# One maximum and one exponential over two PSUM banks in the attention stages of a four-layer megakernel

## The chip, the cores and the metric

The kernel runs on one core of a Trainium2 chip. The metric is the device time of one execution in microseconds. The engines are TensorE (PE; its weight loads are PEld), VectorE (DVE), ScalarE (ACT), GpSimd (POOL) and SyncE (SP). SBUF is the on-chip memory with 128 partitions; PSUM, which PE writes, is used as eight banks of 512 fp32 values in each partition.

## What is computed

Eight sequences of 128 tokens with 128 features pass four layers, each an attention-like part and a feed-forward part with residuals and layer norms. The change touches the three softmax attentions over a context (16 heads of 8 features). All have this core; they differ in what is added to the scores or multiplied to the weights:

```python
# layer 1 (stage A0)
scores = jnp.einsum('bhqd,bhkd->bhqk', q, k) / jnp.sqrt(jnp.float32(DEPTH)).astype(q.dtype)
attn = jax.nn.softmax(scores, axis=-1)
out = jnp.einsum('bhqk,bhkd->bhqd', attn, v)
# layer 2 (stage A1)
logits = logits + neg[:, None, :, :]          # mask, -1e9 where masked
attn = jax.nn.softmax(logits, axis=-1)
attn = attn * group_prob[:, None, :, :]
# layer 3 (stage A2)
scores = jnp.einsum('bhtd,bhsd->bhts', q, k) + bias   # relative position
weights = jax.nn.softmax(scores, axis=-1)
```

## The kernel before

Instructions of each engine stand in one hand-written order, and engines wait for each other by counting semaphores. An attention stage `a` (0, 1, 2; called A0, A1, A2 here) handles the eight sequences as blocks `b` in turn. The 16 heads of a block are four groups `j` of four heads `g`; a group's 4 x 128 scores fill one PSUM bank, and groups go in pairs `p` (j = 2p and 2p+1).

For each block PE computes the scores twice. `att_rows` (L888) gives them with queries on the partitions, into banks 0 and 1, and `att_max` on DVE (L909) takes the negated row maxima, one instruction for each bank. PE transposes the maxima (`att_max_pe`, L940), and DVE adds them to the queries as extra features (`att_max_dve`, L949, tile QX). `att_cols` (L962) then gives the shifted scores with keys on the partitions, into banks 2 and 3, and `att_exp` on ACT (L980) takes the exponential of each bank into PF. `att_pv` (L997, L1003) sums the weights and multiplies them by the values; `att_norm` divides (REC L1011, AT L1015), `att_out` projects, and `att_x` (L1049) adds the result to X. In A0 and A2 the next layer norm is applied by POOL, in A1 by DVE (XN, L306); in A1 and A2 `turn_one_pe` (L349) transposes each normed block for the next layer.

The stages differ so:

- A0 has no mask. The matmuls of a pair's two banks alternate, so both banks are finished almost together.
- A1 adds a mask by two 512-wide matmuls for each bank, all of bank 0 (or 2) before those of bank 1 (or 3); they are issued by a helper and shown as L187 (NMA, NMB with DGH, DGL). The maximum is split into three fp16 parts by five small DVE instructions (`att_max_split`, L919, L921, L923, L925, L927). POOL multiplies each exponentiated bank by the group probabilities (`att_group`, L984).
- A2 adds a position bias by helper matmuls (L187 with FLIP), one for each bank of scores on the row side and two on the column side.

PE's order in a block is: `att_cols` of pair 0, `att_rows` of the next block's pair 1, `att_pv` of the last block's groups 2 and 3, `att_cols` of pair 1, L940 of the next block, `att_out` of block b-2, `att_rows` of block b+2's pair 0, `att_pv` of groups 0 and 1, and the turn of block b-3. PE already waits for both maxima of a pair before it writes banks 0 and 1 again, and for both exponentials before it writes banks 2 and 3 again.

Of the kernel before, what the change touches and what calls it, by code (L numbers as in the profile page):

```python
# [40 lines left out]
def gated_mix_program(nc, t, out):  # L41
# [5 lines left out]
    with ctx:  # L47
# [5 lines left out]
        def sem(name):  # L53
            if name not in sems:
                sems[name] = ctx.enter_context(nc.semaphore(name))
            return sems[name]
# [845 lines left out]

        def att_max(dve, a, b, u, j):

            n = NB * a + b
            dve.wait_ge(sem("a_rows"), 4 * n + j + 1)
            src = bank(j % 2).rearrange("p (g s) -> p g s", g=4)
            dst = MF[:, 0, 4 * j:4 * j + 4] if a == 1 else MB[:, u, :, 32 * j + 24]
            dve.tensor_reduce(dst, src, AX, ALU.max, negate=True).then_inc(sem("a_max"), 1)  # L909

# [62 lines left out]

        def att_exp(act, a, b, u, j):

            n = NB * a + b
            act.wait_ge(sem("a_cols"), 4 * n + j + 1)
            if n:
                act.wait_ge(sem("a_pv"), 4 * n + j - 3)
            act.activation(PF[:, j, :], bank(2 + j % 2), ACT.Exp).then_inc(sem("a_exp"), 1)  # L980

# [112 lines left out]
        def att_act(act, a):  # L1094
            k, j = NEXT[a]
            for b in range(NB):
                u = b % 2
                for i in range(4):
                    att_exp(act, a, b, u, i)
                if b >= 1:  # L1100
                    att_high(act, a, b - 1, 1 - u)
                if j and b >= 3:
                    turn_one_act(act, j, b - 3)
            att_high(act, a, NB - 1, 1)
            if j:
                for b in range(NB - 3, NB):
                    turn_one_act(act, j, b)

        def att_dve(dve, a):
# [8 lines left out]

            for i in range(4):
                att_max(dve, a, 0, 0, i)  # L1120
            att_max_split(dve, a, 0, 0)
            att_max_dve(dve, a, 0, 0)
            for b in range(NB):
                u, end = b % 2, b == NB - 1
                if not end:
                    att_max(dve, a, b + 1, 1 - u, 0)
                    att_max(dve, a, b + 1, 1 - u, 1)
                if own and b >= 2:
# [3 lines left out]
                if not end:  # L1132
                    att_max(dve, a, b + 1, 1 - u, 2)
                    att_max(dve, a, b + 1, 1 - u, 3)
                    att_max_split(dve, a, b + 1, 1 - u)
# [431 lines left out]
```

## Time and profile before

| what | value |
|---|---|
| median of 3 runs | 828.68 us (827.31 to 829.53) |
| the profiled execution's own time | 829.18 us |
| its span, first to last instruction | 827.4 us |
| mean granted clock of TensorE | 0.862 of full |
| PE busy | 662.5 us (80%) |
| DVE busy | 639.3 us (77%) |
| ACT busy | 363.7 us (44%) |
| POOL busy | 357.8 us (43%) |
| chain that ended last | PE 64%, DVE 20%, POOL 8%, issue 6%, ACT 2% |

The busy times are unions over the whole span, in which projection, attention and expert stages with different limits follow each other. The chain is the sequence of work, followed back from the last instruction, that had to be done in that order for the program to end when it did.

### The profile page before, as it was taken

What the parts mean: (1) busy time and instruction counts of PE and PEld (TensorE: products, weight loads), DVE (VectorE), ACT (ScalarE), POOL (GpSimd) and SP (SyncE); (2) the same over time, 40 slices, a digit from 0 to 9 for tenths busy, and PEclk for the clock granted to TensorE, in tenths of its full rate; (3) what the DMA queues carried; (4) which work ended last, traced back from release to release, by engine and by line L of the source; (5) the groups of instructions that cost most, each with busy time, mean ns of one, the idle gap of its engine ahead of it and who ended that gap; (6) DMA issues with size and microseconds to landing.
All of it is one profiled execution on the core that took longest, in us unless ns stands there. A gap on an engine that the chain in (4) does not pass through costs nothing.

```text
span 827.4 us, 17071 instructions
## 1 busy us (share of the span) xinstructions
PE 662.5 (80%) x5144; PEld 317.1 (38%) x5144; DVE 639.3 (77%) x1199; ACT 363.7 (44%) x630; POOL 357.8 (43%) x642
## 2 busy tenths in 40 slices
PE   1359924999988684878993899999999976997696
PEld 0113312444434463324542344444444432454342
DVE  5558764799977786666886799999999967575696
ACT  1314411888875441332331445555555545333443
POOL 6065624577742155205665244554444420025251
PEclk9755555999997798689996899999999988899799
DMA  8000000121204000000000111111111100000110
GB/s 257 0 0 2 0 0 8 44 55 53 55 27 124 2 3 2 1 0 2 2 2 11 33 53 51 52 55 55 53 50 53 55 13 1 2 3 2 32 54 29
DMA packets 46244, 26.81 MB, mean 32 GB/s; under 512 B 17255, under 2 KB 45207, under 8 KB 46032
## 3 DMA queue, kind: packets, MB, share of 16 engines
q1 hardware_dynamic: 44792, 24.36, 10.6%
q10 hardware_dynamic: 1408, 1.85, 0.6%
q8 instruction: 29, 0.48, 0.2%
q14 instruction: 15, 0.12, 0.0%
HBM read 25.63 MB, written 0.56 MB: 32 GB/s over the span
## 4 chain that ended last, share of the span: by engine, by line
PE 64%; DVE 20%; POOL 8%; issue 6%; ACT 2%; DVEq 0%; POOLq 0%; ACTq 0%
PE PS L187 51%; PE PS L446 4%; POOL RSTD L302 4%; DVE SHARED L875 3%; DVE MB L909 2%; PE PS L997 2%; PE PS L888 2%; PE PS L1003 1%; DVE MF L909 1%; POOL VE L300 1%; DVE STAT L290 1%; DVE REC L1011 1%; PE PS L962 1%; DVE XN L306 1%; PE PS L940 1%
## 5 line engine op out<-in xcount | busy, mean ns | idle before, releaser
L709 ACT ACTIVATE SHARED<-SHARED 128x512 f16<-128x512 f32 x180 | 112.4, 630 | 126.8 <-DVE SHARED L724 122.3
L729 DVE TENSOR_TENSOR SHARED<-SHARED 128x512 f16<-128x512 f32 x180 | 145.8, 830 | 12.6 <-ACT SHARED L709 12.2
L724 DVE TENSOR_TENSOR SHARED<-SHARED,PS 128x512 f32<-128x512 f32 x180 | 120.9, 686 | 11.3 <-ACT SHARED L702 7.3
L187 PE MATMUL PS<-XH,UH 128*128 128x512 f16 x296 | 113.9, 385 | 2.2 <-ACT CT L553 2.2
L187 PE MATMUL PS<-XL,UH 128*128 128x512 f16 x296 | 113.8, 384 | 0.0
L187 PE MATMUL PS<-XH,UL 128*128 128x512 f16 x296 | 113.7, 384 | 0.0
L187 PE MATMUL PS<-SHARED,DNH 128*128 128x512 f16 x360 | 107.1, 379 | 5.4 <-DVE SHARED L729 5.3
L980 ACT ACTIVATE SHARED<-PS 128x512 f32<-128x512 f32 x96 | 52.3, 595 | 99.2 <-PE PS L187 74.2
L720 DVE TENSOR_TENSOR SHARED<-SHARED,PS 128x512 f32<-128x512 f32 x116 | 78.7, 679 | 10.7 <-PE PS L187 10.7
L656 POOL CAST DNH<-DF 128x128 f16<-128x128 f32 x90 | 26.0, 289 | 134.6 <-PE PS L187 134.6
L646 POOL TENSOR_TENSOR UL<-UF,UH 128x256 f16<-128x256 f32 (+1 forms) x90 | 69.4, 771 | 7.2
L187 PE MATMUL PS<-CT,SEL 128*128 128x512 f16 x180 | 69.1, 384 | 0.0
L187 PE MATMUL PS<-SHARED,DNL 128*128 128x512 f16 x180 | 68.3, 379 | 0.0
L699 ACT ACTIVATE SHARED<-PS 128x512 f32<-128x512 f32 x116 | 62.3, 584 | 3.9 <-PE PS L187 3.9
L644 POOL CAST UH<-UF 128x256 f16<-128x256 f32 (+1 forms) x90 | 45.5, 506 | 41.4 <-PE PS L187 39.0
L300 POOL TENSOR_SCALAR VE<-MV 128x1 f32<-128x1 f32 x72 | 15.9, 220 | 104.3 <-DVE MV L296 104.2
L984 POOL TENSOR_TENSOR SHARED<-SHARED,GPT 128x512 f32<-128x512 f32 x32 | 40.0, 1271 | 43.7 <-ACT SHARED L980 43.7
L909 DVE TENSOR_REDUCE MB<-PS 128x4 f16<-128x512 f32 x64 | 41.2, 688 | 19.0 <-PE PS L187 13.9
L187 PEld LDWEIGHTS PS<-SHARED,DNH 128*128 128x128 f16 x360 | 34.6, 97 | 49.7 <-issue 13.4
L658 POOL TENSOR_TENSOR DNL<-DF,DNH 128x128 f16<-128x128 f32 x90 | 48.1, 535 | 7.2
L702 ACT ACTIVATE SHARED<-PS,B 128x512 f32<-128x512 f32 x64 | 43.8, 687 | 6.9 <-PE PS L187 1.9
L187 PEld LDWEIGHTS PS<-XH,UH 128*128 128x128 f16 x296 | 29.2, 99 | 44.2 <-issue 11.7
(260 smaller groups left out, 1248.6 us busy)
## 6 DMA issues: line engine op xcount, KB each, us to landing
UF<-in_up SPq DMA_DIRECT2D x58, 128.0 KB, 2.0
DF<-in_down SPq DMA_DIRECT2D x90, 64.0 KB, 1.8
SEL<-in_sel SPq DMA_DIRECT2D x90, 32.0 KB, 1.7
UF<-in_up SPq DMA_DIRECT2D x32, 64.0 KB, 1.7
SHARED<-t_values_dram SPq DMA_DIRECT2D x2, 1024.0 KB, 10.5
SHARED<-in_masks ACTq DMA_DIRECT2D x1, 1024.0 KB, 10.3
WF<-in_wsmall SPq DMA_DIRECT2D x1, 868.0 KB, 6.2
X<-in_x SPq DMA_DIRECT2D x1, 512.0 KB, 3.7
```

The source lines that it names most:

```text
L187: last = pe.matmul(dst, l, r, start=start and i == 0, stop=stop and i == len(pairs) - 1)
L644: pool.tensor_copy(UH[:, u, 0:n], UF[:, u, 0:n]).then_inc(sem("e_up_ready"), 1)
L646: pool.tensor_tensor(UL[:, u, 0:n], UF[:, u, 0:n], UH[:, u, 0:n], ALU.subtract)\
L658: pool.tensor_tensor(DNL[:, u, :], DF[:, u, :], DNH[:, u, :], ALU.subtract)\
L699: act.activation(SG[:, hf, :], bank(hf), ACT.Silu).then_inc(sem("e_act"), 1)
L702: act.activation(SG[:, hf, :], bank(hf), ACT.Relu, bias=B1[:, bass.ds(c, 1)]).then_inc(sem("e_act"), 1)
L709: act.activation(HHI[:, u, hf, :], HF[:, hf, :], ACT.Copy).then_inc(sem("e_high"), 1)
L720: dve.tensor_tensor(TG[:, hf, :], SG[:, hf, :], bank(2 + hf), ALU.mult).then_inc(sem("e_gated"), 1)
L724: dve.tensor_tensor(HF[:, hf, :], src[:, hf, :], bank(4 + hf), ALU.mult).then_inc(sem("e_hidden"), 1)
L729: dve.tensor_tensor(HLO[:, u, hf, :], HF[:, hf, :], HHI[:, u, hf, :], ALU.subtract).then_inc(sem("e_low"), 1)
L909: dve.tensor_reduce(dst, src, AX, ALU.max, negate=True).then_inc(sem("a_max"), 1)
L980: act.activation(PF[:, j, :], bank(2 + j % 2), ACT.Exp).then_inc(sem("a_exp"), 1)
```

## The change

Each pair of banks is read by one instruction. The maximum waits for both banks' scores, reads 128x1024 values and writes 128x8; the exponential waits for both banks of shifted scores and writes 128x1024. Each raises its semaphore by two. All other instructions, and the order on each engine, stay as they are.

```diff
-        def att_max(dve, a, b, u, j):
+        def att_max(dve, a, b, u, p):
 
             n = NB * a + b
-            dve.wait_ge(sem("a_rows"), 4 * n + j + 1)
-            src = bank(j % 2).rearrange("p (g s) -> p g s", g=4)
-            dst = MF[:, 0, 4 * j:4 * j + 4] if a == 1 else MB[:, u, :, 32 * j + 24]
-            dve.tensor_reduce(dst, src, AX, ALU.max, negate=True).then_inc(sem("a_max"), 1)
+            dve.wait_ge(sem("a_rows"), 4 * n + 2 * p + 2)
+            src = bank(0, 2).rearrange("p (j g s) -> p j g s", j=2, g=4)
+            if a == 1:
+                dst = MF[:, 0, :].rearrange("p (j g) -> p j g", j=4)[:, 2 * p:2 * p + 2, :]
+            else:
+                dst = MB[:, u].rearrange("p g (j c) -> p j g c", j=4)[:, 2 * p:2 * p + 2, :, 24]
+            dve.tensor_reduce(dst, src, AX, ALU.max, negate=True).then_inc(sem("a_max"), 2)
...
-        def att_exp(act, a, b, u, j):
+        def att_exp(act, a, b, p):
 
             n = NB * a + b
-            act.wait_ge(sem("a_cols"), 4 * n + j + 1)
+            act.wait_ge(sem("a_cols"), 4 * n + 2 * p + 2)
             if n:
-                act.wait_ge(sem("a_pv"), 4 * n + j - 3)
-            act.activation(PF[:, j, :], bank(2 + j % 2), ACT.Exp).then_inc(sem("a_exp"), 1)
+                act.wait_ge(sem("a_pv"), 4 * n + 2 * p - 2)
+            act.activation(PF[:, 2 * p:2 * p + 2, :].rearrange("p j n -> p (j n)"), bank(2, 2), ACT.Exp).then_inc(sem("a_exp"), 2)
...
                 if not end:
                     att_max(dve, a, b + 1, 1 - u, 0)
-                    att_max(dve, a, b + 1, 1 - u, 1)
                 if own and b >= 2:
                     att_low(dve, a, b - 2, u)
                 if j and b >= 4:
                     turn_one_dve(dve, j, b - 4)
                 if not end:
-                    att_max(dve, a, b + 1, 1 - u, 2)
-                    att_max(dve, a, b + 1, 1 - u, 3)
+                    att_max(dve, a, b + 1, 1 - u, 1)
```

On DVE, in a middle block of stage A1, the order before has two maxima for each pair, MF being the row maxima, MB their fp16 parts and XL the low half of a turned block:

```order
L909 TENSOR_REDUCE MF<-PS 128x4 [waits a_rows] x2
L1030 TENSOR_TENSOR ATL<-AT,ATH 128x128 [waits a_out,a_at_hi]
L357 TENSOR_TENSOR XL<-PS,XH 128x128 [waits xt_high]
L909 TENSOR_REDUCE MF<-PS 128x4 [waits a_rows] x2
L919 TENSOR_SCALAR MB<-MF 128x4x4 [waits a_max]
L921 SCALAR_TENSOR_TENSOR MF<-MB,MF 128x16 [waits a_msplit]
```

The same place of the changed kernel, whose lines are numbered three higher from here on:

```order
L912 TENSOR_REDUCE MF<-PS 128x8 [waits a_rows]
L1033 TENSOR_TENSOR ATL<-AT,ATH 128x128 [waits a_out,a_at_hi]
L357 TENSOR_TENSOR XL<-PS,XH 128x128 [waits xt_high]
L912 TENSOR_REDUCE MF<-PS 128x8 [waits a_rows]
L922 TENSOR_SCALAR MB<-MF 128x4x4 [waits a_max]
L924 SCALAR_TENSOR_TENSOR MF<-MB,MF 128x16 [waits a_msplit]
```

Nothing changes places; of two instructions in a row one is left, of twice the width. On ACT, in the same stage, four exponentials (PS to PF, which lies in SHARED) stand between the copies of the attention output (ATH) before:

```order
L353 ACTIVATE XH<-PS 128x128 [waits xt_turned]
L980 ACTIVATE SHARED<-PS 128x512 [waits a_pv,a_cols] x4
L1022 ACTIVATE ATH<-AT 128x128 [waits a_out,a_norm]
L353 ACTIVATE XH<-PS 128x128 [waits xt_turned]
L980 ACTIVATE SHARED<-PS 128x512 [waits a_pv,a_cols] x4
```

and in the changed kernel there are two of twice the width:

```order
L353 ACTIVATE XH<-PS 128x128 [waits xt_turned]
L983 ACTIVATE SHARED<-PS 128x1024 [waits a_pv,a_cols] x2
L1025 ACTIVATE ATH<-AT 128x128 [waits a_out,a_norm]
L353 ACTIVATE XH<-PS 128x128 [waits xt_turned]
L983 ACTIVATE SHARED<-PS 128x1024 [waits a_pv,a_cols] x2
```

## Rows read from the trace of the kernel before

**Rows 1.** Windows: us, busy (count) of each engine, clock, DMA.

```profile
272.00:319.00 47.00, 36.13 (x822) 26.27 (x822) 36.63 (x74) 19.34 (x39) 20.45 (x37) 0.85 0.01 3
361.00:446.00 85.00, 69.43 (x966) 36.16 (x967) 61.67 (x145) 22.06 (x48) 48.36 (x52) 0.92 0.01 2
377.00:381.00 4.00, 4.00 (x49) 2.10 (x50) 1.81 (x3) 0.00 (x0) 0.00 (x0) 0.57 0.00 0
397.00:414.00 17.00, 16.39 (x250) 8.76 (x246) 14.24 (x35) 5.29 (x12) 11.09 (x11) 1.00 0.01 2
713.00:752.00 39.00, 39.00 (x670) 22.41 (x668) 27.97 (x58) 14.86 (x33) 8.43 (x17) 1.00 0.01 3
```

**Rows 2.** Groups by line: count, busy us, mean ns, idle before.

```profile
L980 ACT ACTIVATE SHARED<-PS 128x512 f32<-128x512 f32 x96 | 52.3, 595 | 99.2 <-PE PS L187 74.2
L909 DVE TENSOR_REDUCE MB<-PS 128x4 f16<-128x512 f32 x64 | 41.2, 688 | 19.0 <-PE PS L187 13.9
```

**Rows 3.** Single lines: ns min/median/max, first and last start.

```profile
L1237 DVE TENSOR_REDUCE AMX<-XN x1: 1220/1220/1220, 325.5 to 325.5; 128x8 f32<-128x1024 f32 x1
...
L790 ACT ACTIVATE SHARED<-PS x3: 1023/1023/1023, 246.2 to 821.1; 128x1024 f32<-128x1024 f32 x3
...
L923 DVE TENSOR_SCALAR MB<-MF x8: 202/204/1227, 365.2 to 426.9; 128x16 f16<-128x16 f32 x8
```

**Rows 4.** The chain that ended last, in A0: start, us, what.

```profile
302.95 1.19 DVE MB L909 x2
...
304.19 0.44 PE PS L888 x8
```

**Rows 5.** Timeline of PE, one block of A1: start, us, instruction, idle before.

```profile
405.27 0.39 PE L962 MATMUL PS<-QX,SHARED 32*128 32x128 f16 x8
...
406.25 0.38 PE L187 MATMUL PS<-NMB,DGL 128*128 128x512 f16 x1
...
407.65 0.38 PE L187 MATMUL PS<-NMA,DGL 128*128 128x512 f16 x1
...
413.60 0.30 PE L349 MATMUL PS<-EYE,XN 128*128 128x128 f32 x1 [0.18 <-DVE X L1049]
413.84 0.40 PE L962 MATMUL PS<-QX,SHARED 32*128 32x128 f16 x8
```

**Rows 6.** Timeline of ACT, the same block.

```profile
406.24 1.08 ACT L980 ACTIVATE SHARED<-PS 128x512 f32<-128x512 f32 x2 [0.59 <-PE PS L187]
```

**Rows 7.** Timeline of POOL, the same block.

```profile
406.91 2.50 POOL L984 TENSOR_TENSOR SHARED<-SHARED,GPT 128x512 f32<-128x512 f32 x2 [0.52 <-ACT SHARED L980]
410.62 2.50 POOL L984 TENSOR_TENSOR SHARED<-SHARED,GPT 128x512 f32<-128x512 f32 x2 [1.20 <-ACT SHARED L980]
```

**Rows 8.** Timeline of DVE, the same block.

```profile
405.35 1.25 DVE L909 TENSOR_REDUCE MF<-PS 128x4 f32<-128x512 f32 x2
...
407.63 1.29 DVE L909 TENSOR_REDUCE MF<-PS 128x4 f32<-128x512 f32 x2 [0.63 <-PE PS L187]
408.96 0.52 DVE L919 TENSOR_SCALAR MB<-MF 128x16 f16<-128x16 f32 x1
...
411.45 0.42 DVE L949 TENSOR_TENSOR QX<-PS,SHARED 128x512 f16<-128x512 f16 x1
411.78 1.42 DVE L306 TENSOR_SCALAR XN<-X,MV,RSTD 128x128 f32<-128x128 f32 x1
```

**Rows 9.** Timeline of DVE, block 0 of A1.

```profile
373.94 1.23 DVE L923 TENSOR_SCALAR MB<-MF 128x16 f16<-128x16 f32 x1
375.20 1.16 DVE L925 SCALAR_TENSOR_TENSOR MF<-MB,MF 128x16 f32<-128x16 f16 x1
```

**Rows 10.** Timeline of POOL, block 0 of A1.

```profile
373.85 2.48 POOL L984 TENSOR_TENSOR SHARED<-SHARED,GPT 128x512 f32<-128x512 f32 x2 [0.22 <-ACT SHARED L980]
```

**Rows 11.** Timeline of ACT, last block of A2.

```profile
753.25 1.09 ACT L980 ACTIVATE SHARED<-PS 128x512 f32<-128x512 f32 x2 [0.59 <-PE PS L187]
```

**Rows 12.** Timeline of PE, last block of A2.

```profile
754.59 0.40 PE L962 MATMUL PS<-QX,SHARED 32*128 32x128 f16 x8
```

More of the change, by code:

```diff
@@ L1097, in att_act @@
                 u = b % 2
-                for i in range(4):
-                    att_exp(act, a, b, u, i)
+                att_exp(act, a, b, 0)
+                att_exp(act, a, b, 1)
                 if b >= 1:
@@ L1117, in residual @@
                 ln_mean(dve, k, b, b)
-            for i in range(4):
-                att_max(dve, a, 0, 0, i)
+            att_max(dve, a, 0, 0, 0)
+            att_max(dve, a, 0, 0, 1)
             att_max_split(dve, a, 0, 0)
```

## The prediction

> **What bounds the kernel now.** I read the windows first, then the chain that ended last, then the timelines of single blocks. The change touches three attention stages, here A0, A1 and A2 (a = 0, 1, 2); A0 takes 47 and A1 85 us of the 827.4 us span. The windows [rows 1] say that they have different limits. In the middle of A2 PE is busy 39.00 of 39.00 us: it is the bound there, and DVE and ACT have air. In A0 PE is busy 36 of 47 us and DVE 37 of 47, and the chain goes through DVE: two maxima, eight score matmuls [rows 4], two maxima again, then the softmax division, QX and the residual, without a gap. In A1 no engine looks full (PE 69, DVE 62, POOL 48 of 85 us), so a loop of waits has to be looked for.
>
> One block of A1 lasts from the `att_cols` matmuls at 405.27 to those of the next block at 413.84: 8.57 us [rows 5]. In it ACT takes its first two exponentials at 406.24 [rows 6], POOL multiplies them by the group probabilities from 406.91 for 2.50 us, to 409.41, and the other two from 410.62 to 413.12 [rows 7]. On DVE [rows 8] the second pair of maxima begins when its bank's mask products are done (407.63) and ends at 408.92; then comes L919, 0.52 us long, to 409.48; XN (L306) takes 1.42 us, to 413.20; after it come X (L1049) and, 0.18 us idle later, PE's transpose L349 and the next block's L962 [rows 5]. Both long instructions end 0.07 to 0.08 us after a pair of POOL's multiplications. In block 0 of this stage it is plainer: L923, 0.204 us in the median [rows 3], takes 1.23 us from 373.94 and L925 after it 1.16 us to 376.36 [rows 9], while POOL multiplies from 373.85 to 376.33 [rows 10]. Each is let through when one POOL multiplication of 1.24 us ends. So in A1 these DVE instructions wait for POOL, and the loop is: cols, exponentials, POOL's first pair, L919, the split, ..., XN held to the end of POOL's second pair, X, turn, cols. That DVE and POOL block each other here is what the trace shows. The Trainium skill, "SBUF — State Buffer", section "Who interferes with whom", names it: a port pair shared by the two, held for a whole instruction, and asked for by DVE's `tensor_scalar` and by forms with two SBUF inputs, but not by a reduce. By that rule the trace agrees.
>
> **The change, part by part.**
>
> *Size of the wide instruction.* A 512-wide maximum takes 688 ns and a 512-wide exponential 595 ns [rows 2]. The 128x1024 reduce L1237 takes 1220 ns, the 1024-wide activation over two PSUM banks L790 1023 ns [rows 3]. L1237 reads SBUF and the maxima PSUM; I take 1.22 for them too, the nearest row, and L790 read PSUM. Two separate maxima overlap at their ends: a ready pair takes 1.25 us, one that had to wait 1.29 [rows 8], a pair of exponentials 1.08 [rows 6]. So a fused pair saves 0.03 to 0.07 us on DVE and 0.06 on ACT, not the 0.156 (2 x 0.688 - 1.22) that the means suggest. The Trainium skill, "Perfetto Trace Analysis", section "Optimizing Scalar/DVE Operations", puts the engine-busy overhead of a DVE instruction on PSUM at about 125 ns; by it A0's 16 pairs would give 2.0 us back (an estimate) where the rows give under 1. The same section says that where these engines are not saturated and make others wait, splitting instructions can finish work sooner, which speaks against this change.
>
> *A0.* Scores of both banks end almost together (the eight matmuls of rows 4 take 0.44 us, so the last two are 0.05 apart). The first pair of a block saves 0.04; the second starts 0.05 later and still saves 0.03. Over 8 blocks 0.56, less about 0.1 in the first blocks where PE runs slower: **-0.4 us**. The bounds are 0 and -2.5 (16 x 0.156).
>
> *A1, exponentials.* Here bank 2's mask products end two products before bank 3's. The first exponential started at 406.24; the last mask product ends at 406.25 + 0.38 = 406.63, so a fused one starts at 406.67, **0.43** later [rows 5, 6]. POOL's first multiplication waits for the first exponential (0.595) now, and for both (1.023) then: **0.43** more. POOL's pair thus starts and ends **0.86 us later**: 407.77 to 410.27. L919 is then ready at 409.3 and is let go at 410.33 instead of 409.48, so the split, REC, AT and QX all move by 0.85. The second exponentials and POOL's second pair move by the same 0.86, since `att_cols` for it hangs on PE's order and not on DVE. QX ended at 411.87 and the first of that POOL pair ended at 411.87 too (410.62 + 1.25), and XN lost that race; both sides move equally, so I take it that XN loses again and ends at 414.06. X, turn and the next cols follow: the block costs **+0.86**. In blocks 1 and 2 there is no XN yet, but the loop closes through L919, PE's L940, the next row scores and the value products: again +0.86. Block 0 is alike (POOL's two pairs back to back) at about +0.9; in block 7 the four multiplications run back to back from the first exponentials to the final value products: +0.86. Sum 0.9 + 6 x 0.86 + 0.86 = 6.9.
>
> *A1, maxima.* The fused maximum waits for the last mask product: 407.65 + 0.38 = 408.03 in place of 407.63, and ends at 409.27 in place of 408.92, **+0.35**. That hides in all blocks behind the 0.86 at L919 (behind DVE's wait for POOL, that is; without it +0.35 would show). Only block 0's own maxima, ahead of the first exponential, are uncovered: +0.35, less 0.06 for the pair before: +0.3. **A1 in all: +7.2 us.** Queued behind DVE's late maxima are the split and so PE's L940, counted above; queued behind POOL's late pair is ln_rstd, which waits for the residual's mean, itself 0.86 later.
>
> *A2.* The mask here is one product a bank on the row side, 0.22 us (half of the two products' 0.43), so a waiting maximum ends 0.22 - 0.07 = 0.15 later; on the column side it is two, so the pair of exponentials ends 0.43 - 0.06 = 0.37 later. PE waits for neither in the 39 us in which it is full. Exposed are block 0's maxima, when PE has nothing else (+0.15, less 0.05 for the pair before), and the last block: its fused exponentials would begin at 753.25 + 0.43 and end at 754.70 [rows 11], while L962, which needs both, starts at 754.59 [rows 12]: +0.1. **+0.2 us.**
>
> **Sum.** -0.4 + 7.2 + 0.2 = +7.0 us. The profiled execution took 829.18 us, 1.8 of it outside the span, where nothing changes; with the sum it is 836.2. This execution lies 0.5 above the median of 828.68, so **835.7 us** (+0.84%). A measurement of this kernel can tell about 0.3%, 2.5 us.
>
> **The rivals.**
>
> *POOL's delay is free* (0.10). If L919 and XN are long for another reason than POOL, only the late maxima count: 8 x 0.35 - 0.05 x 8 in A1, so 2.4 - 0.4 + 0.2 = +2.2, 830.9 us. For it: it is the plain reading of the chain, which names DVE and not POOL. Against it: four long instructions of rows 8 and 9 each end within 0.08 us of a POOL end.
>
> *The wide maximum saves a whole fixed cost* (0.04). If DVE saves the upper bound, 0.156 a pair, A0 gives 2.5 back instead of 0.4 and A1 and A2 gain nothing, being held elsewhere: 833.6. Against it stands the overlap of the pairs in rows 8. The 125 ns of "Perfetto Trace Analysis" in the Trainium skill is this case, by its own figure.
>
> *XN wins its race* (inside my forecast). If QX ends a hair before POOL's first multiplication, XN no longer waits. PE then becomes the limit: L940 is still 0.86 late and PE loses only its 0.18 us of idle time [rows 5], so +0.68 in four blocks: 835.0.
>
> *The TensorE clock falls* (0.12). In A1's steady part PE is busy 16.39 of 17 us at clock 1.00; just before, 377 to 381, it ran at 0.57, mostly the lower of its two levels (1.2 and 2.4 GHz), after waiting for the split [rows 1]. With 0.86 us more idle in each block such stretches may come again; one costs about 4.00 x 0.43 = 1.7 us. One to three: 837.4 to 840.8. Against it: A0 waits a larger share of its time and is mostly at 1.00 (0.85 over the stage).
>
> *Faster* (0.04): the later PE work falls into stretches of full clock. The low clock costs now (1 - 0.85) x 47 = 7.0 us of clock in A0 and (1 - 0.92) x 85 = 6.8 in A1 [rows 1], partly off the path. If the shifts made it vanish wholly in both, 835.7 - 13.8 = 821.9; it decides from 9.5 us up, more than two thirds of it. What lies ahead of each stage, and so the start of the slow stretches, doesn't change, so this is remote.
>
> **How the numbers follow.** 0.70 for the forecast, whose own range is 834 to 837; 0.10 for POOL's delay free, 0.12 for the clock, 0.04 each for the fixed cost and for faster. The range reaches down to the second and up into the third: 830.5 to 839.0. The chance of no change (within 2.5 us) takes most of POOL's delay free and a little of shifts that cancel, 0.09; faster 0.04; slower 0.87.
>
> **What would show it.** In the changed profile: the maximum at 1.22 us and the exponential at 1.02; in A1 POOL's pair starting 2.50 us after the block's cols in place of 1.64, L919 lasting about 1.0 us and ending 0.07 after POOL, XN still near 1.4 us, blocks of 9.4 us in place of 8.57, PE idle about 0.9 us before L940; A2's blocks unchanged with PE full; A0's blocks 0.07 shorter. Wrong would make it: L919 short while POOL works, exponentials much longer than 1.02 over two banks, a clock under 1.00 in A1's later blocks.

## The result, and the profile after

The changed kernel takes 845.84 us in the median of 6 runs (843.29 to 847.48), the kernel before 829.08 (827.31 to 829.57). The ratio is 1.0203 with an interval of 1.0183 to 1.0223: slower by 16.8 us, where 7.0 were forecast and the range ended at 839.0. The profiled execution of the changed kernel took 847.17 us with a span of 845.4, so 18.0 us more span than the one of before.

The windows of the changed kernel that answer to [rows 1] (two blocks of A1, and the middle of A2; columns as there):

```profile
404.25:422.17 17.92, 15.53 (x235) 8.27 (x233) 14.36 (x29) 4.99 (x7) 10.77 (x10) 1.00 0.01 2
...
728.00:767.00 39.00, 39.00 (x658) 21.93 (x650) 25.96 (x43) 13.08 (x19) 8.43 (x17) 1.00 0.01 2
```

TensorE is still full in the middle of A2 and loses 2.39 of 17.92 us in A1, at full clock. The new instructions, by line (ns min/median/max, first and last start) and from the page's groups (busy, mean ns):

```profile
L922 DVE TENSOR_SCALAR MB<-MF x8: 203/1056/1130, 367.4 to 435.7; 128x16 f16<-128x16 f32 x8
...
L983 ACT ACTIVATE SHARED<-PS 128x1024 f32<-128x1024 f32 x48 | 49.1, 1023 | 104.1 <-PE PS L187 65.3
...
L912 DVE TENSOR_REDUCE MB<-PS 128x8 f16<-128x1024 f32 x32 | 39.2, 1225 | 23.6 <-PE PS L187 17.4
```

Maximum and exponential have the sizes taken from [rows 3]: 1225 and 1023 ns. L922 is the old L919; its median went to 1056 ns. The same block as in [rows 5 to 8], on PE:

```profile
412.74 0.40 PE L965 MATMUL PS<-QX,SHARED 32*128 32x128 f16 x8
...
418.81 0.40 PE L943 MATMUL PS<-EYEH,MB 128*128 128x128 f16 x4 [1.05 <-DVE MB L930]
...
422.17 0.40 PE L965 MATMUL PS<-QX,SHARED 32*128 32x128 f16 x8
```

on ACT:

```profile
414.19 1.02 ACT L983 ACTIVATE SHARED<-PS 128x1024 f32<-128x1024 f32 x1 [1.07 <-PE PS L187]
```

on POOL:

```profile
415.29 2.50 POOL L987 TENSOR_TENSOR SHARED<-SHARED,GPT 128x512 f32<-128x512 f32 x2 [1.43 <-ACT SHARED L983]
418.94 2.50 POOL L987 TENSOR_TENSOR SHARED<-SHARED,GPT 128x512 f32<-128x512 f32 x2 [1.15 <-ACT SHARED L983]
```

and on DVE:

```profile
415.56 1.22 DVE L912 TENSOR_REDUCE MF<-PS 128x8 f32<-128x1024 f32 x1 [1.13 <-PE PS L187]
416.81 1.04 DVE L922 TENSOR_SCALAR MB<-MF 128x16 f16<-128x16 f32 x1
...
419.83 0.41 DVE L952 TENSOR_TENSOR QX<-PS,SHARED 128x512 f16<-128x512 f16 x1
420.16 1.37 DVE L306 TENSOR_SCALAR XN<-X,MV,RSTD 128x128 f32<-128x128 f32 x1
```

The block lasts 422.17 - 412.74 = 9.43 us instead of 8.57. POOL's first pair starts 2.55 us after the block's cols (1.64 before) and ends at 417.79; L922 ends at 417.85, the split's last part (L930) releases L943, and PE has stood idle 1.05 us for it. XN, asked for at 420.16, ends at 421.53, beside POOL's end at 421.44. That is the loop of the prediction, nearly to the hundredth. Eight blocks of it explain less than half of the loss.

**Where the rest is.** Both programs issue the same 5144 matmuls in the same order, so the start of each can be compared. The table gives, for matmuls named by their start in the trace of before, how much later they start in the changed kernel:

| start before | what it is | shift, us |
|---|---|---|
| 45.70 | L411, the 27th matmul, in the first layer | +0.90 |
| 248.12 | end of the first expert stage | +1.18 |
| 273.60 | A0 begins | +2.33 |
| 321.33 | A0 has ended | +2.39 |
| 362.44 | A1 begins | +2.25 |
| 386.07 | L940 of A1's block 2 | +5.67 |
| 441.31 | A1 has ended | +11.02 |
| 666.10 | end of the second expert stage | +11.89 |
| 684.89 | projection ahead of A2 | +11.15 |
| 694.24 | nine us on in that projection | +13.47 |
| 700.43 | A2 begins | +13.36 |
| 750.10 | A2, full part | +16.51 |
| 822.20 | end | +17.99 |

A1 gives 8.8 of it. But 2.3 stand ahead of A1's start, 2.3 between A1 and A2, 3.2 in A2's first block and 1.5 from there to the end. What stands ahead of A1 need not belong to the change: at 45.70 the same matmul is between 1.66 us early and 0.90 late in the traces at hand, and e13 below, which is the kernel before up to the end of A1, enters A1 2.66 us late. A1 has such a scatter too. e4, e13, e14 and e15 leave it as it was and take -0.1, -2.5, -0.1 and +0.5 us for it, against the trace of before; the -2.5 stand in its first block.

Two of these places can be read. The projection ahead of A2, the same 31 matmuls of the changed kernel and then of the kernel before:

```profile
696.05:707.71 11.66, 9.68 (x31) 3.96 (x32) 7.17 (x11) 5.66 (x9) 0.00 (x0) 0.66 0.00 0
```

```profile
684.89:694.24 9.35, 7.35 (x31) 3.43 (x32) 6.54 (x10) 5.29 (x8) 0.00 (x0) 0.83 0.00 0
```

The granted clock was 0.66 here against 0.83, and the same work took 2.31 us more: more of it was done at the lower of TensorE's two levels (1.2 in place of 2.4 GHz). No instruction of this stage differs. In the stretch just ahead of it (from 666.10 to 684.89 in the kernel before) it is the other way round, again the changed kernel first:

```profile
677.99:696.04 18.05, 7.88 (x56) 4.18 (x54) 10.96 (x34) 6.45 (x10) 6.14 (x16) 0.93 0.01 2
```

```profile
666.10:684.89 18.79, 10.56 (x56) 6.33 (x55) 11.06 (x34) 6.45 (x10) 6.14 (x16) 0.81 0.01 2
```

With two levels, full and half, the time at the lower one is twice the missing share of the clock: 2.5 + 7.9 us in the changed kernel and 7.1 + 3.2 before, so about 10 us over both stretches in either (an estimate). The low clock did not last longer here, it lay later. In the first stretch that gave 0.74 us back, in the projection it cost 2.31. The other place is ACT at the start of A2, in the changed kernel:

```profile
721.09 1.28 ACT L983 ACT_TABLE_LOAD   x1 [9.28 <-issue]
722.38 1.02 ACT L983 ACTIVATE SHARED<-PS 128x1024 f32<-128x1024 f32 x1
725.20 1.02 ACT L983 ACTIVATE SHARED<-PS 128x1024 f32<-128x1024 f32 x1 [1.80 <-issue]
```

and in the kernel before:

```profile
698.40 1.28 ACT L980 ACT_TABLE_LOAD   x1
706.19 0.60 ACT L980 ACTIVATE SHARED<-PS 128x512 f32<-128x512 f32 x1 [6.50 <-PE PS L187]
```

ACT loads the function table of the exponential once at this place, 1.28 us. Before, it did so at 698.40, right behind its last projection work and 6.5 us ahead of need. In the changed kernel it idles 9.28 us first, ahead of the load, and the load then stands between the finished scores and the exponential. PE's next `att_cols` waits for it:

```profile
723.46 0.40 PE L965 MATMUL PS<-QX,SHARED 32*128 32x128 f16 x8 [1.58 <-ACT SHARED L983]
```

The trace's full list of ACT instructions shows why. It prints the semaphore instructions too (start, us, operation, line, semaphores waited for by `>=` and raised):

```
kernel before
697.46  0.02 EVENT_SEMAPHORE L979  S[192]>=
698.40  1.28 ACT_TABLE_LOAD  L980
706.19  0.60 ACTIVATE        L980  S[191]>=  S[150]++
changed kernel
710.93 10.13 EVENT_SEMAPHORE L982  S[192]>= S[191]>=
721.09  1.28 ACT_TABLE_LOAD  L983
722.38  1.02 ACTIVATE        L983  S[150]+=
```

S[191] is `a_cols`, S[192] `a_pv`, S[150] `a_exp`. Before, S[191] stands on the exponential itself: the wait for the scores was part of it, behind the table load. In the changed kernel the exponential raises its semaphore by two, carries no wait any more, and both waits lie in an instruction of their own ahead of the table load. The Trainium skill, "Trainium Kernel Development and Optimization", section "Key Constraints", says that compute semaphores are to be raised by 1; it gives no reason, and here the two did work, at this price.

### The profile page after: what moved, and what is told of

The parts are those of the page before. It is cut to its first block and busy times, and to the rows that moved or that the text cites. A ratio compares the mean times of both kernels' runs of the same rounds, so it can differ in the third digit from the quotient of the medians.

```text
span 845.4 us, 16979 instructions
## 1 busy us (share of the span) xinstructions
PE 667.2 (79%) x5144; PEld 316.5 (37%) x5144; DVE 641.6 (76%) x1151; ACT 362.8 (43%) x582; POOL 354.4 (42%) x642
## 5 line engine op out<-in xcount | busy, mean ns | idle before, releaser
L983 ACT ACTIVATE SHARED<-PS 128x1024 f32<-128x1024 f32 x48 | 49.1, 1023 | 104.1 <-PE PS L187 65.3
L646 POOL TENSOR_TENSOR UL<-UF,UH 128x256 f16<-128x256 f32 (+1 forms) x90 | 65.9, 733 | 7.2
L699 ACT ACTIVATE SHARED<-PS 128x512 f32<-128x512 f32 x116 | 62.7, 588 | 5.4 <-PE PS L187 5.4
L912 DVE TENSOR_REDUCE MB<-PS 128x8 f16<-128x1024 f32 x32 | 39.2, 1225 | 23.6 <-PE PS L187 17.4
```

What stands on the lines that cost most here:

```text
L646: pool.tensor_tensor(UL[:, u, 0:n], UF[:, u, 0:n], UH[:, u, 0:n], ALU.subtract)\
L699: act.activation(SG[:, hf, :], bank(hf), ACT.Silu).then_inc(sem("e_act"), 1)
L983: act.activation(PF[:, 2 * p:2 * p + 2, :].rearrange("p j n -> p (j n)"), bank(2, 2), ACT.Exp).then_inc(sem("a_exp"), 2)
```

## The experiments

All ratios are to runs of the kernel before on the same chip, whose medians were 828.83 to 829.76 us.

**One kind of instruction at a time.** e1 fuses only the maxima, e2 only the exponentials, each in all stages; `att_max` or `att_exp` then calls the old form for both banks:

```diff
         def att_exp(act, a, b, p):
+            if a not in ():        # e1; e2 has this in att_max
+                att_exp_one(act, a, b, 2 * p)
+                att_exp_one(act, a, b, 2 * p + 1)
+                return
```

> Only the maxima are fused, in all three stages; every exponential reads one bank as before. Theory (the cost is the late exponentials: POOL's multiplications and with them DVE in A1, a displaced wait and an uncovered table load in A2): in A1 the fused maximum ends at about 0.35 us later, still before POOL's first pair ends, so L919 is let go at the same moment and the blocks stay at 8.57 us; only block 0 pays 0.3; A0 gains 0.4. In all 829 to 830 us. Rival (the maxima's late start is what costs): 8 x 0.35 in A1 and 0.15 in each block of A2, 832 us or more.

Measured: 830.52 us (828.52 to 832.93), ratio 1.0006 [0.9986, 1.0026]. The wide maxima cost nothing that can be measured and gain nothing. A1's blocks were 8.51 us. The theory holds.

> Only the exponentials are fused, in all three stages. Theory: nearly the whole cost of the change, 842 to 846 us, with A1's blocks at 9.4 us and the ACT table load of A2 behind the wait. Rival (both halves of the change are needed for the loss): under 838 us.

Measured: 838.46 us (833.37 to 842.14), ratio 1.0101 [1.0064, 1.0137]. The exponentials alone cost 8.4 us by the ratio: less than the theory's 842 to 846, and just above the rival's 838. In its trace A1 grew by 5.6 us and A2's first block by 3.9, the table load standing behind the wait there too. A block of A1 was 9.00 us, not 9.43, and XN was not held. DVE and POOL in this kernel:

```profile
412.32 0.29 DVE L934 TENSOR_SCALAR MB<-MF 128x16 f16<-128x16 f32 x1
412.65 1.16 DVE L936 SCALAR_TENSOR_TENSOR MF<-MB,MF 128x16 f32<-128x16 f16 x1
...
415.90 0.34 DVE L306 TENSOR_SCALAR XN<-X,MV,RSTD 128x128 f32<-128x128 f32 x1
```

```profile
411.29 2.50 POOL L1011 TENSOR_TENSOR SHARED<-SHARED,GPT 128x512 f32<-128x512 f32 x2 [2.06 <-ACT SHARED L1007]
414.89 2.50 POOL L1011 TENSOR_TENSOR SHARED<-SHARED,GPT 128x512 f32<-128x512 f32 x2 [1.11 <-ACT SHARED L1007]
```

Here the maxima end 3.56 us after the block's cols, at 412.29, and the first split instruction (L934, the old L919) still passes, in 0.29 us. The second (L936, the old L921) is held to POOL's end at 413.79, and three of the split are left behind it. In the changed kernel the maximum ends 4.04 us after the cols, the first one is held, and four are left. So XN, which came 1.01 us after the start of POOL's second pair here and ran in 0.34, came 1.22 us after it there and was held to the end. The two fusions are not independent. A block takes 8.57 us before, 8.51 with the maxima fused, 9.00 with the exponentials fused, and 9.43 with both: the wide maximum is free by itself and costs 0.43 us beside the wide exponential.

**One stage at a time.** e3 is changed in A1 alone, e4 in A0 and A2 alone:

```diff
+            if a not in (1,):      # e3, in att_max and att_exp; e4: (0, 2)
```

> Both instructions are fused in A1 alone. Theory: A1 costs 7 to 9 us as in the changed kernel, and A0, A2 and what lies between do not move: 836 to 839 us. Rival (the loss outside A1 comes from A1 being longer, by clock stretches that fall elsewhere): 842 us or more.

Measured: 841.91 us (840.99 to 843.92), ratio 1.0156 [1.0128, 1.0183]. That is 12.9 us, well above the theory's 836 to 839 and a hair under the rival's 842 or more; the rival's loss outside A1 is there. In its trace A1 itself grew by 8.6 us; 2.3 more came in the unchanged projection ahead of A2.

> Both instructions are fused in A0 and A2, and A1 is as before. Theory: A0 gives at most 0.5 us back, A2 costs 2 to 4 us, most of it in its first block, by the table load that now stands behind the wait and a second low-clock stretch after it: 831 to 835 us. Rival (the surplus of the changed kernel over the forecast is clock noise of A1's length): 829 us.

Measured: 832.16 us (829.66 to 832.97), ratio 1.0025 [1.0009, 1.0040], 2.1 us. That is within the theory's 831 to 835, and the interval (0.7 to 3.3 us) leaves out the rival's 829. A2's first block lost 1.2 us, with the table load behind the wait as in the changed kernel; another 1.2 came behind A2's full part.

**The increment.** e5 is the changed kernel with one line each for the signal, and all waits counted in pairs:

```diff
-            ....then_inc(sem("a_exp"), 2)
+            ....then_inc(sem("a_exp"), 1)
...
-                pe.wait_ge(sem("a_exp"), 4 * n + 2 * p)
+                pe.wait_ge(sem("a_exp"), 2 * n + p)
```

> The changed kernel, with each fused instruction raising its semaphore by one instead of two, and all who wait for it counting pairs. Nothing else differs. Theory (the increment of two makes both waits of the exponential a separate step on ACT's queue, so that the table load of the exponential in stage A2 waits for block 0's column scores instead of running ahead of them): the table load lies more than 5 us ahead of A2's first exponential again, that exponential starts 1.28 us earlier, and the time falls by 1.3 to 4 us against the changed kernel's 845.8, to 841.8 to 844.5. Rival (what is lost at A2's start is a matter of the clock alone): 845 to 847, the same as the changed kernel. A1's blocks stay at 9.4 us by both.

Measured: 841.50 us (838.30 to 843.09), ratio 1.0138 [1.0113, 1.0162] against 1.0203 with the increment of two: 4.3 us by the medians, 5.4 by the ratios. ACT at A2's start:

```profile
709.43 1.28 ACT L983 ACT_TABLE_LOAD   x1
718.16 1.02 ACT L983 ACTIVATE SHARED<-PS 128x1024 f32<-128x1024 f32 x1 [7.45 <-PE PS L187]
```

The load runs 7.45 us ahead of need again, and A2's first block adds 0.3 us instead of 3.2. The load's place is as the theory had it, and the time lies just under its 841.8 to 844.5. But the 4.3 to 5.4 us are not the load's alone. In e5's trace the projection ahead of A2 takes 9.39 us at 0.83, as in the kernel before, so 2.2 us of the changed kernel's loss are absent ahead of the load. And the same edit on another kernel (e12 against e11, below) gained 0.5 us by the medians and nothing by the ratios.

**POOL out of A1.** e6 and e7 are the two kernels without the multiplication by the group probabilities:

```diff
-                    for j in range(4):
-                        att_group(pool, b, j)
...
-            src = PG if a == 1 else PF
+            src = PF
```

> Left out: in stage A1 the multiplication of the exponentials by the group probabilities on POOL; the value matmuls read the exponentials themselves. Otherwise the kernel before. It is the base for the next run. Theory (DVE's long instructions in A1 wait for POOL): L919 0.20 us in every block and XN 0.34 us; A1's blocks shorter than 8.57 us, at 8.2 us or less, where TensorE is the bound; the time 3 to 6 us under the kernel before. Rival (they are long for another reason): L919 and XN as long as before, 0.52 and 1.42 us, and the time as before.

> Left out: in stage A1 the multiplication of the exponentials by the group probabilities on POOL, as in the run before. Otherwise the changed kernel. Theory (the fused exponential costs A1 its 0.87 us a block only by way of POOL's late multiplications and DVE's wait for them): A1's blocks are longer than in the base by 0.35 us at most, so that the whole is 2 to 6 us above the base, with what A0 and A2 cost. Rival (the lateness of the fused instructions costs it without POOL): 0.86 us a block stays and the whole is 10 to 17 us above the base.

Measured: e6 824.24 us (823.05 to 825.44), e7 829.14 (827.05 to 831.29): the whole change costs 4.9 us without POOL's work, 16.8 with it; in the traces A1 grows by 3.1 us without it, 8.8 with it. In e7, by line:

```profile
L922 DVE TENSOR_SCALAR MB<-MF x8: 203/204/204, 367.8 to 425.0; 128x16 f16<-128x16 f32 x8
```

and PE at two blocks' starts:

```profile
404.28 0.40 PE L965 MATMUL PS<-QX,SHARED 32*128 32x128 f16 x8
...
409.47 0.40 PE L943 MATMUL PS<-EYEH,MB 128*128 128x128 f16 x4 [0.22 <-DVE MB L930]
...
412.65 0.40 PE L965 MATMUL PS<-QX,SHARED 32*128 32x128 f16 x8
```

L922 is 203 or 204 ns in every block and XN 0.34. A block is 8.37 us; in e6 it is 7.97 (398.93 to 406.90). The 0.40 left fit the late maximum, the +0.35 that the prediction had hidden behind the 0.86: it ends 3.99 us after the block's cols, 3.56 in e6, and PE is idle 0.22 us for the split, in e6 not at all. What the late exponential adds to it was not separated. e6 also says what POOL's multiplications cost the kernel before: 4.9 us in all (ratio 0.9941 [0.9919, 0.9963]). In its trace A1 is 8.8 us shorter, 4.1 of them in its first block and 0.6 in each steady one, and 2.3 come back in the projection ahead of A2 and 1.3 behind A2.

**The lateness without the width.** e9 is the kernel before, in which the four single exponentials of A1 wait for both banks:

```diff
-            act.wait_ge(sem("a_cols"), 4 * n + j + 1)
+            act.wait_ge(sem("a_cols"), 4 * n + (2 * (j // 2) + 2 if a == 1 else j + 1))
```

> The kernel before, four separate exponentials a block as there; only in stage A1 each waits until both banks of its pair are written. It takes the lateness of the fused exponential's start without its width. Theory (the 0.86 us of a block are 0.43 for the later start and 0.43 for the longer instruction): POOL's first pair starts 0.43 later, L919 lasts 0.95 us instead of 0.52, blocks of 9.0 us instead of 8.57, the whole 3.5 us above the kernel before, 832 to 835. Rival (the width is what costs, and the later start is absorbed): L919 stays at 0.5 to 0.6 us and the time within 1.5 us of before.

Measured: 832.97 us (830.69 to 835.86), ratio 1.0039 [1.0021, 1.0057], 3.2 us. DVE in a block whose cols start at 407.88 and the next block's at 416.88:

```profile
411.57 0.95 DVE L919 TENSOR_SCALAR MB<-MF 128x16 f16<-128x16 f32 x1
...
414.82 1.42 DVE L306 TENSOR_SCALAR XN<-X,MV,RSTD 128x128 f32<-128x128 f32 x1
```

L919 at 0.95 us and a block of 9.00 us, both as expected. POOL's first pair starts 2.08 us after the cols, where it is 1.64 before and 2.55 in the changed kernel: the wait for the second bank and the wider instruction each delay POOL by about half. The block does not follow in halves as simply. e2 has both the wait and the width, and its blocks are 9.00 us as well, because XN passes there; the second 0.43 comes only with the wide maximum beside it.

**XN in POOL's pause.** e8 is the kernel before and e11 the changed kernel, with XN moved:

```diff
+                if own and b >= 3:
+                    ln_apply(dve, k, b - 3, b - 3, b - 3)
                 if b >= 1:
                     att_norm(dve, a, b - 1, 1 - u)
                 if not end:
                     att_max_dve(dve, a, b + 1, 1 - u)
-                if own and b >= 3:
-                    ln_apply(dve, k, b - 3, b - 3, b - 3)
```

> The kernel before with one move on DVE in stage A1: XN (L306) of block b-3 stands ahead of the softmax division of block b-1, not behind the division and QX, so that it is ready while POOL is idle between its two pairs. Theory (XN waits for POOL): XN takes 0.34 us instead of 1.42, but REC, AT and QX start 0.3 us later; blocks of 8.57 us become shorter by up to 0.4 us where XN stands in them (four or five blocks), 0 to 2 us in all, so 827 to 829.7. Rival (XN's wait is off the path or moves to another instruction): 829 to 831, with QX or REC longer or PE waiting for QX.

> The changed kernel with XN moved ahead of the softmax division in A1. Theory (XN waits for POOL's second pair in the changed kernel, 1.37 us, as it did before): XN at 0.34 us, the five blocks that have it at about 9.0 us instead of 9.42, 1.5 to 3 us less than the changed kernel's 845.8: 842.5 to 844.5. Rival (L922 alone sets the block, and the 0.34 us now stand on the path ahead of QX): blocks of 9.4 to 9.7 us and 845 to 848.

Measured: e8 831.11 us (829.45 to 833.49), ratio 1.0023 [1.0010, 1.0035]; e11 838.53 (838.35 to 840.90), ratio 1.0105 [1.0081, 1.0129]. XN is 0.34 us in both. e8's blocks are 8.33 us, and A1 is 1.8 us shorter in its trace, yet 2.3 come back in the projection ahead of A2 and 1.3 behind A2: a gain in A1 turned into a loss of the whole. The time is at the rival's 829 to 831, but not for its reason, since the blocks did get shorter. e11's blocks are 9.24 us and A1 grows by 7.3 us instead of 8.8; but the whole falls by 7 to 8 us, where 1.5 to 3 were expected. Neither size fits a count of A1's time alone. e11's trace lacks the 2.2 us in the projection ahead of A2 (9.21 us at 0.84), which is part of the difference.

**In search of a better kernel.** e10 has e1's and e8's edits together.

> The maxima fused in all three stages, the exponentials one for each bank, and XN moved ahead of the softmax division in A1. In search of a version better than both kernels. Theory (moving XN saved 1.8 us in A1 in its own trace and lost them to the clock elsewhere; fused maxima cost nothing): A1 1.5 to 3 us shorter, the whole 827 to 830. Rival (either is given back at the clock): 830 to 832.

Measured: 831.72 us (827.40 to 833.73), ratio 1.0020 [1.0001, 1.0039]. A1 is 0.9 us shorter and the whole is not, as the rival had it. No version here with all the work in it beats the kernel before.

**Both repairs.** e12 is the changed kernel with the edits of e5 and e8.

> The changed kernel with both repairs: each fused instruction raises its semaphore by one (waits counted in pairs), and XN stands ahead of the softmax division in A1. Theory (the two losses are separate): 4.3 and 7.3 us less than 845.8, so 834.2, within 832 to 836. Rival (both had gained from the same stretches of low clock, so that the second gives less): 836.5 to 839. In A1 blocks of 9.24 us with XN, as in the run before with XN moved alone; the table load ahead of A2's first exponential.

Measured: 838.01 us (835.75 to 839.17), ratio 1.0105 [1.0078, 1.0132]: no faster than with XN moved alone. The rival had this right: the repairs do not add up. Its reason fits the traces in part. The changed kernel loses 2.2 us in the projection ahead of A2, and e5, e11 and e12 all lack that loss (-0.2 to 0.0 in the table below), so each repair alone had already gained it.

**A plain delay.** In e13, e14 and e15 the kernel before gets 6, 13 and 17 more DVE instructions in the routing behind A1, whose result nobody reads:

```diff
+                for _ in range(6):     # e14: 13, e15: 17
+                    step(dve.tensor_reduce(ZS[:, 3, :], lk, AX, ALU.add))
                 dve.wait_ge(sem("r_exp"), m)
```

> The kernel before with 6 more DVE instructions in a row in the routing behind A1 (sums over 128x512 values of LK into a row of ZS that is overwritten later), 0.72 us each, of which 0.8 us hide behind DVE's wait for L551: a plain delay of 3.5 us at a place where every engine waits for DVE, and nothing else. Theory (a shift of the later stages costs more or less than itself, by where TensorE's low clock falls on them): the time off the 3.5 us by 1 us or more, in either direction, and in the trace the shift changing by 1 to 2.5 us in the projection ahead of A2 or in the tail. Rival (a shift costs just itself): 3.5 us, within 0.7 of it, here and in the next two.

> As the run before, with 13 such instructions: a plain delay of 8.6 us, as long as what the changed kernel loses in A1. Theory (low clock at other places): 10 to 12 us over the kernel before, with 1 to 2.5 us of it in the projection ahead of A2. Rival (a shift costs just itself): 8.6 us, within 0.7 of it.

> As the run before, with 17 such instructions: a plain delay of 11.5 us, about the shift with which the changed kernel enters the projection ahead of A2 in its trace (11.9). Theory (low clock at other places): 13 to 15 us over the kernel before, with 2.3 us of it in the projection. Rival (a shift costs just itself): 11.5 us, within 0.7 of it.

Measured, with the delay as the traces show it (the shift of the matmul at 463.00 less that at 441.31), and what the whole took by the ratio, times 829.1:

| kernel | delay in the trace | the whole, us | ratio | over before | over the delay |
|---|---|---|---|---|---|
| e13 | 3.9 | 832.32 | 1.0036 [1.0020, 1.0052] | +3.0 | -0.9 |
| e14 | 8.9 | 840.71 | 1.0140 [1.0113, 1.0167] | +11.6 | +2.7 |
| e15 | 12.0 | 846.26 | 1.0202 [1.0175, 1.0228] | +16.7 | +4.7 |

The intervals are 1.3 us wide either way for e13 and 2.2 for e14 and e15. So the short delay costs itself, within the noise, and the two long ones cost more than themselves, by 2.7 and 4.7 us. In e14's trace the projection ahead of A2 shows the clock of the changed kernel, not that of the kernel before:

```profile
691.68:703.45 11.77, 9.79 (x31) 4.01 (x32) 7.28 (x11) 5.66 (x9) 0.00 (x0) 0.66 0.00 0
```

For e14 the theory holds, in size and in place: 2.4 us come in the projection, 1.3 in A2's first block and 0.7 behind it, with no instruction of them changed. In e15's trace the projection is at 0.82 and takes 9.50 us; that execution, 843.18 us, is the lowest of its six, the others are 845.47 to 846.45, and behind the delay it loses nothing more. So the 16.7 us of the medians lie above the theory's 13 to 15, and no trace shows where the surplus over the delay falls. e13's 3.0 us is the rival's (3.5, within 0.7), and its trace shows no step behind the delay.

The shifts in the traces, in us, at matmuls named by their start before:

| kernel | 273.60 | 362.44 | 441.31 | 684.89 | 700.43 | 750.10 | 822.20 |
|---|---|---|---|---|---|---|---|
| changed | 2.33 | 2.25 | 11.02 | 11.15 | 13.36 | 16.51 | 17.99 |
| e1 | 0.01 | 0.04 | 0.43 | 0.46 | 0.26 | 0.65 | 1.31 |
| e2 | -0.07 | -0.56 | 5.04 | 5.03 | 5.54 | 9.43 | 9.59 |
| e3 | -0.11 | -0.47 | 8.15 | 8.37 | 10.67 | 10.47 | 11.81 |
| e4 | 1.92 | 1.34 | 1.25 | 1.27 | 1.15 | 2.37 | 3.57 |
| e5 | 1.17 | 0.64 | 10.72 | 10.99 | 10.97 | 11.31 | 12.16 |
| e6 | -0.31 | -1.07 | -9.82 | -9.57 | -7.26 | -7.46 | -6.12 |
| e7 | 2.76 | 2.60 | -3.02 | -2.53 | -0.15 | 1.32 | 2.11 |
| e8 | -1.48 | -1.66 | -3.42 | -3.21 | -0.88 | -1.06 | 0.28 |
| e9 | 1.74 | 0.94 | 4.43 | 3.82 | 3.95 | 4.01 | 4.03 |
| e10 | 0.46 | -1.38 | -2.31 | -2.47 | -1.98 | -1.49 | -1.41 |
| e11 | 0.01 | 0.03 | 7.29 | 7.17 | 6.97 | 8.18 | 9.33 |
| e12 | -1.72 | -1.62 | 5.34 | 5.48 | 5.29 | 5.58 | 6.37 |
| e13 | 2.58 | 2.66 | 0.15 | 4.03 | 4.09 | 4.12 | 4.13 |
| e14 | -1.46 | -1.83 | -1.88 | 6.79 | 9.16 | 10.46 | 11.15 |
| e15 | 1.61 | 2.10 | 2.57 | 13.75 | 13.91 | 13.98 | 14.00 |

The step between 684.89 and 700.43, where no kernel differs, is -0.2 to 0.5 us in ten of the sixteen rows and 2.2 to 2.4 in six. One trace is one execution of each, so these rows place a loss, and the medians above size it.

**A2's first block, taken apart.** The matmuls from 700.43 to 713.15 of the kernel before, in nine traces:

| kernel | table load | length, us | granted clock |
|---|---|---|---|
| before | ahead of need | 12.72 | 0.73 |
| e5, e12 | ahead of need | 13.07, 13.02 | 0.74, 0.74 |
| e14 | ahead of need | 14.02 | 0.63 |
| e4, e7, e11 | behind the wait | 13.94, 14.20, 13.94 | 0.76, 0.76, 0.76 |
| changed | behind the wait | 15.87 | 0.68 |
| e2 | behind the wait | 16.61 | 0.59 |

At a clock near that of before, the load behind the wait costs 0.9 to 1.2 us (e4, e7 and e11 against e5 and e12), no more than its own 1.28. The changed kernel's 15.87 are 1.7 to 1.9 more than that, at a lower clock. e14 shows that a lower clock alone can lengthen this block, by 1.3 us there.

## Why the prediction was wrong in size

The direction and the loop were right, the size was not: +16.8 for +7.0, more than twice what was forecast. What failed is the term of the sum for everything outside the three stages, put at nothing, and the term for A2, put at 0.2.

- **Sizes of the wide instructions**: right, 1225 and 1023 ns. What fusing saves was right too: nothing that shows, neither the 0.156 us a pair nor the 125 ns of the Trainium skill. "Perfetto Trace Analysis" in the Trainium skill, section "Optimizing Scalar/DVE Operations", speaks of engine-busy overhead, and e1 shows that 48 fewer maxima leave the time where it was, in A0 too, where the chain went through DVE (shifts 0.01 at its start and 0.04 at A1's).
- **A0, -0.4**: its shift is 2.33 at the start and 2.39 behind it, so 0.0 to 0.1. Within the traces' spread.
- **A1, +7.2**: 8.8 in the trace. The block is 0.86 longer, as forecast. POOL's delay has the two halves that the prediction gave it (e9), and e6 and e7 confirm the way through POOL. But the split between the terms was wrong, and that the sum was right is luck in part. The prediction gave all 0.86 to the exponentials and hid the maxima. With the exponentials alone fused XN passes and the block grows by 0.43 (e2); the late maximum brings the rest. The six steps from 386.07 to 436.48 give 5.28, 0.88 each. The prologue's maxima gave 0.44 for 0.3. The step from 366.51 to 386.07, which spans two blocks, gives 2.98 (2.69 to 5.67) for 1.8. In its first block three split instructions of DVE in a row are held, as the rows of the changed kernel below show; in the kernel before two were, L923 and L925 [rows 9]. The granted clock between these two matmuls was 0.77 against 0.81 before, so a part of this may be the rival of the clock. It was not separated, and most of it looks like the loop: the second block takes 9.36 us for 7.80, in e2 9.30 and in e9, without the width, 8.23.

```profile
376.10 1.13 DVE L922 TENSOR_SCALAR MB<-MF 128x16 f16<-128x16 f32 x1
377.26 1.25 DVE L924 SCALAR_TENSOR_TENSOR MF<-MB,MF 128x16 f32<-128x16 f16 x1
378.54 1.21 DVE L926 TENSOR_SCALAR MB<-MF 128x16 f16<-128x16 f32 x1
```

- **XN**: loses in the changed kernel, as taken; it wins in e2, where the maxima are single. The prediction priced that at 0.18 us in each of four blocks; e2's blocks are 0.43 us shorter than the changed kernel's.
- **POOL's delay free**, 830.9: false. The cost falls from 16.8 to 4.9 us with POOL's work left out.
- **A2, +0.2**: a term was missing. The sum had read the increment of two as a matter of counting. It takes the wait out of the exponential and puts it ahead of the table load, and that costs 0.9 to 1.2 us in the traces. The first block lost 3.2 us in the changed kernel's trace: 0.3 stay with the load ahead of need (e5, e12), where 0.1 was forecast for that block, and what is left goes with a lower clock. By the time of the whole the increment costs 4.3 to 5.4 us in one pair of kernels (e5) and 0.5 or nothing in another (e12 against e11).
- **What lies outside the three stages, nothing**: this is the step that failed most. The prediction priced the lower clock only where A1's own idle time might call it up, and set the rest aside with "what lies ahead of each stage, and so the start of the slow stretches, doesn't change". The changed kernel's trace has 2.3 us between A1 and A2 and 1.5 behind A2's full part, where only A2's last block has changed instructions (e3 has none there, and its trace still loses 1.3). The delay runs show that a shift can change what lies behind: 8.9 us of pure delay cost 11.6, 12.0 cost 16.7. The changed kernel loses 8.8 us in A1; a delay of that length gives 11.6 (e14), and the change in A1 alone 12.9 (e3). With the 2.1 of A0 and A2 alone (e4) that is 15.0, against the measured 16.8; the difference is inside the intervals (2.3, 1.3 and 1.7 us either way).

What stays open: why one shift puts the low clock on the projection and on A2's first block, and another does not, is not settled. Each kernel has one trace, so it is not shown either that all its executions do the same. The excess over the delay is shown by medians; that it is the clock is shown by windows over the same matmuls in the changed kernel and in e14 (0.66 against 0.83 in the projection, 0.68 and 0.63 against 0.73 in A2's first block). Behind A2's full part it was 0.88 against 0.91 in the changed kernel, over 73.6 and 72.1 us. For e15 it is only argued.

## What to carry to other kernels

Before two instructions on two banks are made one, look at who waits for the first of them alone: here POOL did, whose multiplications hold DVE up, and its start was delayed twice, once by the later start of the exponential and once by its longer run. Test two fusions together as well as apart: here one was free alone and cost 0.43 us a block beside the other. Raise compute semaphores by one and count pairs in the waits, or look where the waits lie in the queue afterwards. And do not price a loss of several microseconds at itself when TensorE's clock is low in parts of the span: give it a factor in the range, here 1.0 to 1.4 by plain delays.

## What the runs showed of the hardware

- POOL's multiplications hold single DVE instructions up (that DVE holds POOL up as well, as the prediction has it, no row shows: each of POOL's multiplications takes 1.26 to 1.34 us in the traces of the kernel before and the changed one), and there is a narrow gap between two of POOL's. L922 (16 values in a partition, 204 ns alone) took 1.02 to 1.13 us in seven of eight blocks while POOL multiplied, and 203 or 204 ns in all eight with POOL's work out. XN is 0.34 us long alone. It took 0.34 or 0.35 us when it came 1.01 to 1.09 us after the start of the first of a pair of POOL's 1.25 us multiplications (e2, and one block each of the changed kernel and e3), and 1.37 to 1.44 when it came 1.15 to 1.22 after (the kernel before, changed, e3 to e5, e9, e13 to e15). The Trainium skill, "SBUF — State Buffer", section "Who interferes with whom", has the rule for whole instructions, and the trace agrees; that 0.06 us (1.09 or 1.15) decide between passing and waiting for a whole further instruction is what these runs add.
- An increment of two moved ACT's wait for `a_cols` out of its instruction (one separate semaphore instruction of 10.13 us ahead of the table load, for 0.02 before). The table load itself is 1.28 us in all traces, and in the changed kernel the exponential follows 0.01 us behind it. The Trainium skill, "ScalarE: Activation LUTs", section "What ACT_TABLE_LOAD costs", gives 1283 ns, which agrees, and a drain of 1380 ns more, which no row here shows.
- A saving of 1.8 us in A1's trace (e8) ended as a loss of 1.4 to 1.9 us, and a delay of 12.0 us as one of 16.7, with no instruction of the later stages changed. About 10 us at the lower clock lay ahead of A2 in the kernel before and in the changed one, and cost 1.6 us more where more of it fell on the projection.
